# Second cross attention of a two-layer Perceiver block: probabilities turned by VectorE in 32x32 squares and moved by transfers inside SBUF, in place of TensorE transposes

## What is computed

```python
xq   = layernorm(x)                                    # (8, 64, 256)
q    = (xq @ w_q).reshape(B, 64, 16, 64)
k, v = ctx @ w_k, ctx @ w_v                            # ctx: (8, 1024, 256)
attn = softmax(einsum('bhqd,bhkd->bhqk', q, k) * 64 ** -0.5)
out  = einsum('bhqk,bhkd->bhqd', attn, v)
x    = x + out.reshape(B, 64, 1024) @ w_o
```

## Time and profile before

| | us |
|---|---|
| median of the three executions | 1008.06 |
| the profiled execution, first to last instruction | 1008.6 |
| of it, the second block of `xattn1` up to its last values (424.50 to 844.85) | 420.35 |
| the rest of that block (844.85 to 865.86) | 21.01 |
| TensorE busy in the whole execution | 963.9 |
| VectorE busy | 552.4 |
| ScalarE busy | 497.9 |
| GpSimd busy | 180.9 |

### The profile page before, as it was taken

The page is one execution under the profiler, slowest core; times in us unless marked ns, Lnnn a source line. Parts: engine busy times, 40 slices in busy tenths (PEclk is TensorE's granted clock), DMA queues, the critical chain, the costliest instruction groups (busy, mean ns, idle before and its releaser), DMA issues. The chain is left out here.

```text
span 1008.6 us, 21010 instructions
## 1 busy us (share of the span) xinstructions
PE 963.9 (96%) x8772; PEld 798.4 (79%) x8772; DVE 552.4 (55%) x800; ACT 497.9 (49%) x716; POOL 180.9 (18%) x188
## 2 busy tenths in 40 slices
PE   8999999888899999899999999999999999997997
PEld 7888887665689985589999999998989996657554
DVE  5677777666443354565646465646464642367212
ACT  4777776353656645554444454454444532321331
POOL 2000000022224423012121212121212101421101
PEclk9999999899989999999999999999999999999999
DMA  5211110022023304111111111111113000599994
GB/s 154 86 47 47 47 47 5 2 63 65 2 84 94 94 22 167 37 48 43 43 43 42 42 42 42 42 42 42 42 58 140 0 1 1 133 332 310 336 328 143
DMA packets 57366, 84.55 MB, mean 84 GB/s; under 512 B 5506, under 2 KB 46163, under 8 KB 57299
## 3 DMA queue, kind: packets, MB, share of 16 engines
q1 hardware_dynamic: 56466, 81.22, 25.5%
q0 software_dynamic: 832, 2.36, 0.8%
HBM read 80.94 MB, written 2.62 MB: 83 GB/s over the span
## 5 line engine op out<-in xcount | busy, mean ns | idle before, releaser
L186 PE MATMUL ps<-f_pT_hi,f_cN_hi 128*128 128x256 f32 x512 | 145.4, 284 | 0.0
L186 PE MATMUL ps<-f_pT_hi,f_cN_lo 128*128 128x256 f32 x512 | 144.7, 283 | 0.0
L186 PE MATMUL ps<-f_pT_lo,f_cN_hi 128*128 128x256 f32 x512 | 144.7, 283 | 0.0
L1596 ACT ACTIVATE e_pr<-ps,e_negmax 128x1024 f32<-128x1024 f32 x64 | 71.5, 1116 | 129.9 <-DVE e_negmax L1601 127.6
L1870 DVE TENSOR_TENSOR f_pT_lo<-ps,f_pT_hi 128x1024 fp32r<-128x1024 f32 x64 | 78.3, 1224 | 81.8 <-ACT f_pT_hi L1808 81.6
L186 PE MATMUL ps<-e_cT_hi,e_qb_hi 128*128 128x512 f32 (+1 forms) x288 | 115.4, 401 | 0.0
L186 PE MATMUL ps<-e_cT_hi,e_qb_lo 128*128 128x512 f32 (+1 forms) x288 | 109.8, 381 | 0.0
L186 PE MATMUL ps<-e_cT_lo,e_qb_hi 128*128 128x512 f32 (+1 forms) x288 | 109.1, 379 | 0.0
L1808 ACT CAST f_pT_hi<-ps 128x1024 fp32r<-128x1024 f32 x64 | 64.9, 1014 | 84.6 <-PE ps L1920 83.8
L445 DVE SCALAR_TENSOR_TENSOR a_u<-ps,a_floor,a_cap 128x1024 f32<-128x1024 f32 x64 | 79.2, 1279 | 48.3 <-PE ps L540 47.9
L186 PEld LDWEIGHTS ps<-f_pT_hi,f_cN_hi 128*128 128x128 f32 x512 | 97.8, 191 | 2.6 <-issue 0.8
(11 more groups left out here) (401 smaller groups left out, 1961.0 us busy)
## 6 DMA issues: line engine op xcount, KB each, us to landing
k_w<-in_L_ffn_W SPq DMA_DIRECT2D x30, 1024.0 KB, 13.3
a_ctxT<-in_ctxT SPq DMA_DIRECT2D x16, 512.0 KB, 4.5
d_w<-in_L_ffn_w SPq DMA_DIRECT2D x32, 256.0 KB, 2.7
e_raw<-in_ctxT SPq DMA_DIRECT2D x8, 1024.0 KB, 5.0
e_raw<-in_ctx SPq DMA_DIRECT2D x8, 1024.0 KB, 5.8
k_b<-in_L_ffn_b SPq DMA_DIRECT2D x14, 256.0 KB, 11.8
k_w<-in_L_xattn_w_q SPq DMA_DIRECT2D x1, 1024.0 KB, 5.1
e_wk<-in_L_xattn_w_k SPq DMA_DIRECT2D x1, 1024.0 KB, 7.6
```

The source lines that it names most:

```text
L186: last = nc.tensor.matmul(out, a[i], b[j], start=start and n == 0, stop=stop and n == 2, skip_group_check=skip)
L1596: nc.scalar.activation(pr[:, p % NPR, :], core.ps[p % 2][:], ACT.Exp, bias=negmax[:, p:p + 1], accum_out=total[:, p:p + 1]).then_inc(exp_r ...
```

## The change

The eight transposes of a part on TensorE, and the PSUM tile that they filled, are gone. Instead VectorE turns the divided probabilities in 32x32 squares (`turn`, one instruction for the 128x1024 of a part, written to `f_turned`). A square is then right in itself, but stands in the wrong one of the four groups of 32 partitions. So SyncE moves the squares (`move`): 16 transfers a group of two parts, each from 32 partitions of `f_turned` to 32 partitions of `f_pT_lo`, 2 KB a partition, 64 KB in all. The tile `f_turned` exists once; `f_pT_lo` and `f_pT_hi` exist twice.

After the move ScalarE casts `f_pT_lo` to `f_pT_hi` in two halves (`high`), and the difference is written back into `f_pT_lo`, half of it by GpSimd and half by VectorE (two functions `low`), from SBUF operands. The outputs read the moved tiles as [p, r, i, q], in runs of 32 columns. The context's positions are dealt to partitions to suit (`load_keys` has four transfers in place of one). Probabilities before the turn live in `xn` and `xnT`, the transposed context has two buffers, and w_v and w_o are loaded into the raw context's tiles, in the last batch. All batches are written out; there is no loop.

```diff
         def load_keys(sp, b):
-            sp.dma_start(raw[:], one(a["ctx"], b).rearrange("(k p) d -> p k d", p=P)).then_inc(n_in, 16)
+            for j in range(4):
+                sp.dma_start(raw[QD * j:QD * j + QD, :, :], a["ctx"][b, S // 4 * j:S // 4 * (j + 1), :].rearrange(
+                    "(m k) d -> k m d", k=QD)).then_inc(n_in, 16)
...
             @block.sync
-                for b in range(1, B):
-                    sp.wait_ge(t_hi, 2 * b)
-                    sp.wait_ge(t_lo, 4 * b)
-                    load_features(sp, b)
-                    sp.wait_ge(n_hi, 2 * b)
-                    sp.wait_ge(n_lo, 4 * b)
-                    load_keys(sp, b)
+                def move(G):
+                    sp.wait_ge(turned_ready, 2 * G + 2)
+                    if G >= 2:
+                        sp.wait_ge(o_psum, 2 * (G - 2) + 2)
+                    for j in range(4):
+                        for i in range(4):
+                            sp.dma_start(pT_lo[G % 2][QD * j:QD * j + QD, i, :, :, :].bitcast(F32),
+                                         turned[QD * i:QD * i + QD, j, :, :, :]).then_inc(pT_in[G % 2], 16)
...
             @block.gpsimd
+                def low(G):
+                    pool.wait_ge(hi_ready, 2 * G + 1)
+                    half = pT_lo[G % 2][:, 0:2, :, :, :].rearrange("p i r m q -> p (i r m q)")
+                    nc.gpsimd.tensor_tensor(half, half.bitcast(F32), pT_hi[G % 2][:, 0:2, :, :, :].rearrange(
+                        "p i r m q -> p (i r m q)").bitcast(F32), ALU.subtract).then_inc(lo_pool, 1)
...
             @block.scalar
+                def high(G):
+                    act.wait_ge(pT_in[G % 2], MOVES * (G // 2 + 1))
                     for i in range(2):
+                        nc.scalar.copy(pT_hi[G % 2][:, 2 * i:2 * i + 2, :, :, :].rearrange("p i r m q -> p (i r m q)"),
+                                       pT_lo[G % 2][:, 2 * i:2 * i + 2, :, :, :].rearrange("p i r m q -> p (i r m q)")
+                                       .bitcast(F32)).then_inc(hi_ready, 1)
...
+                for b, g in groups:
+                    G = NG * b + g
+                    if G >= 1:
+                        exponentials(2 * G)
+                        high(G - 1)
+                    if g == 0 and b >= 1:
+                        queries(b, 1)
+                    if g == 1 and b >= 1:
+                        keys(b, 0)
+                    if g == 2 and b + 1 < B:
+                        features(b + 1, 0)
+                    exponentials(2 * G + 1)
+                    if G >= 2:
+                        outputs(G - 2)
...
             @block.vector
+                def turn(n):
+                    G, r = n // 2, n % 2
+                    if r == 0 and G >= 1:
+                        dve.wait_ge(pT_in[(G - 1) % 2], MOVES * ((G - 1) // 2 + 1))
+                    dve.wait_ge(p_ready, n + 1)
+                    nc.vector.transpose(turned[:, :, r, :, :].rearrange("p j m q -> p j (m q)"),
+                                        pr[n % NPR].rearrange("p (j s) -> p j s", j=4)).then_inc(turned_ready, 1)
...
+                for b, g in groups:
+                    G = NG * b + g
+                    if G >= 1:
+                        dve_maximum(dve, b, 2 * g)
+                        dve_divide(dve, b, 2 * g)
+                    turn(2 * G)
+                    if g == 1 and b >= 1:
+                        dve_queries(dve, b, 1)
+                    if g == 3 and b + 1 < B:
+                        dve_queries(dve, b + 1, 0)
+                    dve_maximum(dve, b, 2 * g + 1)
+                    if G >= 1:
+                        low(G - 1)
+                    dve_divide(dve, b, 2 * g + 1)
+                    turn(2 * G + 1)
...
             @block.tensor
-                    for k in range(KT):
-                        last = nc.tensor.transpose(core.ps[2][:, k * P:(k + 1) * P],
-                                                   pr[:, p % NPR, k * P:(k + 1) * P], core.ident[:])
-                    last.then_inc(pT_psum, 1)
...
+                    if G >= 1:
+                        pe_scores(pe, b, 2 * g)
+                    if G >= 3:
+                        outputs(G - 2, 0)
+                    if G >= 1:
+                        pe_scores(pe, b, 2 * g + 1)
+                    if G == 2:
+                        outputs(0, 0)
+                    if G >= 2:
+                        outputs(G - 2, 1)
```

More of the change, by code:

```diff
@@ L1751, in xattn1 @@
             y_psum, x_out, x_stats = sem("y_psum"), sem("x_out"), sem("x_stats")
+            MOVES = 16 * 16
+            groups = [(b, g) for b in range(B) for g in range(NG)]
             block = inner.enter_context(nc.Block())
@@ L1803, in high @@
[L1803 to L1816 removed]
+                    if b >= 2:
+                        act.wait_ge(s_psum, HP * (b - 1))
@@ L1857, in _ @@
-                high(0, 0)
-                exponentials(0, 1)
-                exponentials(0, 2)
-                each(act, B, batch)
-                for p in range(1, HP):
+                keys(0, 0)
+                keys(0, 1)
+                for b, g in groups:
+                    G = NG * b + g
[5 more added lines that the diff above has]
+                    if g == 1 and b >= 1:
+                        keys(b, 0)
+                    if g == 2 and b + 1 < B:
+                        features(b + 1, 0)
+                    exponentials(2 * G + 1)
+                    if G >= 2:
+                        outputs(G - 2)
+                    if g == 1 and b >= 1:
+                        keys(b, 1)
+                    if g == 2 and b + 1 < B:
+                        features(b + 1, 1)
+                        queries(b + 1, 0)
@@ L1862, in _ @@
+                act.wait_ge(v_in, 32)
+                nc.scalar.copy(wo2[0], wo).then_inc(wo_hi, 1)
+                attended(0)
+                attended(1)
+                high(NG * B - 1)
+                outputs(NG * B - 2)
+                attended(2)
+                attended(3)
+                outputs(NG * B - 1)
+                for p in range(4, HP):
                     attended(p)
@@ L1898, in _ @@
-                dve_maximum(dve, 0, 1)
-                each(dve, B, batch)
-                for p in range(HP):
+                def turn(n):
[5 more added lines that the diff above has]
+                                        pr[n % NPR].rearrange("p (j s) -> p j s", j=4)).then_inc(turned_ready, 1)
```

267 lines of the change are left out of this document (108 added, 159 removed).

## The result

The changed kernel takes **1226.01 us** (median of four executions, 1225.68 to 1227.23). The kernel before, run beside it, took 1007.98. The ratio is 1.216, with a 95% interval of 1.214 to 1.218: 218 us slower. The forecast was 1127, with a range of 1060 to 1195. The sign and the mechanism came out, the size did not, and the time lies above the range.

A forecast was written before the change was run, and what follows sets the result against it. TensorE's own work bounded the second `xattn1` block (419.00 of 420.35 us). Afterwards a loop through `f_turned` sets the pace: 5.8 + 31 x 16.6 + 19.1 = 539.5, +119.2 on 1008.06, so 1127 us, range 1060 to 1195.

The forecast's parts named there:

- D: Time from a group's second turn's end to its sixteen transfers' landing: 9.2 us, bounds 7.2 and 10.4.
- rest of the group: From the move's landing to the end of the next group's second turn: mean 7.4 us.
- last second turn to the block's end: Landing, first cast, GpSimd's half of `low`, last outputs, copy and hops: 19.1 us, then an unchanged 21.01.
- the layers behind the block: Work after the block's end, forecast at 142.7 us.
- the price of one issue: Each transfer's start on SyncE's queue: 0.49 us, from twelve issues in a row; the sixteenth starts after 7.35.
- The high end: Top of the range: D = 10.4 from 0.51 us an issue, with 1.6 us a turn, 602 for the block, rounded to 1195.
- The outputs' 32-column runs: TensorE's outputs reading runs of 32 columns: counted as free, 0.12 us between matmuls.
- The rival of the cheap move: Issues overlap and the move costs only its bytes: D = 4.5, kernel 977 us; 8 in 100.
- The rival of slow transfers: Transfers at 0.75 us each: D = 13.1, kernel 1252 us; 11 in 100 for times above range, slow turns included.
- The slow turn: VectorE turns of 2.44 us would give 1203 us; a page-based estimate of 2.49 us a turn gave 1206.
- The clock: Rival: TensorE's stalls leave half clock lasting, kernel 1326 us, 4 in 100; a short drop is hidden by idle time.
- Its rule: The kernel gets faster only below D = 5.5, where the block is again 420 us; needs under 0.25 us an issue.

The follow-up runs named there:

- e10: Changed kernel with moves on two queues and VectorE's and TensorE's orders changed, plus all of `low` on VectorE, none on GpSimd: 998.64 us.
- e1: Changed kernel with the same bytes moved by 32 transfers of 32 KB a group in place of 16 of 64 KB: 1551.77 us.
- e2: Changed kernel with 8 transfers of 128 KB a group in place of 16 of 64 KB, squares landing in wrong places: 1072.89 us.
- e12: e10 unchanged, timed again beside the kernel before the change: median of six 993.09 us, ratio 0.983.
- e3: Changed kernel with one transfer of 1 MB over 128 partitions a group in place of 16 of 64 KB, values not the reference's: 1016.68 us.

## Why the prediction was right in kind and short in size

The forecast's span was 1008.6 + 119.2 = 1127.8; the measured one is 1224.2. The 96.4 us between them, by the steps of the prediction:

| step | forecast | measured | us |
|---|---|---|---|
| start to the end of the first group's second turn | at 430.3 | at 431.88 | +1.6 |
| D, 31 times | 9.2 | 11.76 | +79.4 |
| rest of the group, 31 times | 7.4 | 7.58 | +5.3 |
| last second turn to the block's end | 40.1 | 46.4 | +6.3 |
| the layers behind the block | 142.7 | 146.6 | +3.9 |

**The step that failed is the price of one issue**, 0.49 us from twelve loads from memory. It measured 0.591, and 0.63 with the gap between two. That is 15 x 0.14 = 2.1 of the 2.56 us. The landing took 2.0 in place of 1.8. The last 0.25 are single long issues, of up to 1.63 us, in some groups. The loop multiplies every one of these by 31. The twelve issues were also not a whole series: the same queue issues without a pause from 866.27 to beyond 879.00, with the 1.78, 0.58, 1.15, 1.84 and 0.64 us shown above on either side of the twelve. Over that whole stretch an issue comes every 0.71 us (12.73 / 18), and 15 x 0.71 would have given D = 12.5. The row was read right, but the calm part of a series stood for all of it. The high end had the same fault: 0.51 was the longest of the twelve, taken without the 0.04 between two issues, as a bound for transfers of a kind that no row showed. With 0.63 and 2.0 the same formula gives D = 11.5 and 1201, so the range's top of 1195 was too low by the spread of this one unknown. I had left 11 in 100 for times above it.

**The rest of the group was right**, 7.4 against 7.58, and so was its make-up. In the group shown, the turn takes 1.25 (1.2 in the forecast), GpSimd's half 2.35 (2.4). VectorE's half starts early and ends at 621.69, 4.56 after the landing (4.6), since it waits inside the instruction for GpSimd's (in e10, with nothing on GpSimd beside it, it takes 1.255). The division took 1.58 beside GpSimd, as in the earlier trace rows. The second turn ends 7.53 after the landing; g = 1 has 8.4 and g = 2 7.4 (7.9 for both in the forecast), g = 0 6.7 (6.7), g = 3 7.7 (7.0).

**The outputs' 32-column runs cost nothing**, as forecast. In the timeline of the last outputs, once the clock is back, matmuls start 0.12 us apart, as before.

**The rival of the cheap move** is out: issues do not overlap, and e1 and e2 show that their number sets the time. The Trainium skill, *DMA: Bandwidth & Descriptors*, section *Issuing engines are not separate DMA queues*, calls the sequencer's time usually small beside the transfer; here sixteen issues take 10.1 us and the same 1 MB in one transfer lands in 5.2. **The rival of slow transfers** described what happened, in half its size: it had 0.75 an issue. **The slow turn** did not come. The estimate of 2.49 us, from eight times the 311 ns that the Trainium skill, *VectorE: DVE Perf Modes*, section *The three transpose paths*, gives, is double the 1.245 measured.

**The clock** did what the rival's last sentence said. In each group it falls behind TensorE's stall, to a mean of 0.55 and 0.59 (618 to 624 and 600 to 606 in the windows), which is mostly the lower level of 1.2 GHz, and is back at 1.00 in the long stretch (606 to 616). Within the loop this is hidden: it makes TensorE busy for the 70 us more, but VectorE has no wait for TensorE in the block. At the end of the block it is not, and that is part of the +6.3. The windows around the last outputs, which ran alone, and their first matmuls:

```profile
1049.00:1051.00 2.00, 2.00 (x12) 2.00 (x11) 0.45 (x1) 0.00 (x0) 0.00 (x0) 0.50 0.34 119
1053.00:1056.00 3.00, 2.87 (x24) 2.65 (x22) 0.00 (x0) 0.10 (x1) 0.00 (x0) 1.00 0.00 0
```

```profile
1048.36 0.36 PE L186 MATMUL ps<-f_pT_hi,f_cN_hi 128*128 128x256 f32 x1 [4.96 <-issue]
...
1049.70 0.41 PE L186 MATMUL ps<-f_pT_lo,f_cN_hi 128*128 128x256 f32 x1
1049.91 0.41 PE L186 MATMUL ps<-f_pT_hi,f_cN_lo 128*128 128x256 f32 x1
...
1052.44 0.28 PE L186 MATMUL ps<-f_pT_hi,f_cN_hi 128*128 128x256 f32 x1
1052.56 0.28 PE L186 MATMUL ps<-f_pT_lo,f_cN_hi 128*128 128x256 f32 x1
```

TensorE stood still for 4.96 us; then its matmuls are 0.21 apart and from 1052 on 0.12. The 48 take 7.5 us in place of 5.74 (+1.8). The last landing came 12.55 after the turn in place of 9.2 (+3.35), and the outputs began 4.65 after it in place of 3.4 (+1.25), since VectorE's `low` ran 2.52 us to 1048.25. The forecast had counted only GpSimd's half here, though its own walk through the loop has VectorE's half end 4.6 after the landing.

**The layers behind the block** are 3.9 us longer, with the same work. Windows of before and of after:

```profile
865.86:1008.60 142.74, 128.80 (x766) 79.36 (x766) 58.16 (x145) 41.17 (x68) 30.68 (x46) 0.97 0.90 279
```

```profile
1077.57:1224.20 146.63, 129.45 (x766) 80.60 (x766) 58.09 (x145) 41.19 (x68) 30.67 (x46) 0.96 0.90 272
```

TensorE is busy for 0.65 us more and idle for 3.2 more, while the DMA engines have the same share. In the traces of e1 to e12 these layers take 144.5 to 147.8 us, whatever the block took (146.95 in e3, whose block ended at 867.7), so it is not the later hour. Whether the place of the weight loads in the queue does this was not tried, and before has a single trace.

**What the prediction left thin** is how cheap the move would have to be for the change to pay. Its rule says below D = 5.5. e3 had D = 5.21 and a period of 12.87, under the 13.04 before, and its block still took 443.8 us where 441.4 were needed, for the start and the end of the block are longer; with the layers behind it the kernel took 1016.68. The order was taken as given as well, though 7.4 of the 16.6 us were in it.

## What to carry to other kernels

Count transfers before bytes: where a loop waits for a series of small transfers on one queue, it costs the number of issues times the measured price of an issue of that kind, times the number of rounds, and a second queue takes its share off at once. Give a term that a loop multiplies by 31, and that no row shows, a range as wide as its kind could be, not as narrow as the nearest series. Look at what stands on either side of the rows that you pick, too: here the trace before held the dearer issues right beside the twelve. And when a wait closes a loop, ask of each instruction between the two ends whether it must stand there: moving the maximum, the subtraction and the division out here was worth 131 us, nearly as much as halving the number of transfers (153).

## What the runs showed of the hardware that I had not expected

- An issue of a transfer from SBUF to SBUF in a series takes 0.591 us on SyncE's queue and 0.617 on ScalarE's, for 32, 64 and 128 KB, for 32 partitions and (0.601) for 128. The first of a series takes 0.51 (0.47 over 128 partitions), the second on ScalarE's queue 0.87. Loads from memory behind such a series were 0.51 apart.
- A transfer inside SBUF lands no sooner than one from memory: 1.9 us after its issue for 32 KB, 2.0 for 64 (from memory 1.8), 2.4 for 128, 5.2 for 1 MB (from memory 5.0 in the kernel after).
- A VectorE turn of 128x1024 fp32 in 32x32 squares takes 1.245 us, with little spread (1.196 to 1.250 in all kernels), as much as a maximum or a subtraction over 1024 columns (the division takes 0.75). GpSimd never drew it out: 48 of the 64 turns of the kernel after ran beside a GpSimd instruction, and none of them took over 1.247.
- Splitting a subtraction of SBUF tiles between VectorE and GpSimd gains almost nothing for VectorE: 2.2 us for its half beside GpSimd, 2.5 for the whole alone.
